# The gated block of a four-block convolution kernel: positions on partitions for the softplus, the delta by rank, two norms side by side

## The reference

```
xn = LN(x) * norm_w + norm_b                      # over the channels of a position
x1, x2 = halves of xn @ w_in.T
xss, z = silu(halves of x1 @ ssm_in_w.T)
xd = xss @ x_proj_w[k].T                          # per direction k = 0..3: 8 dt ranks, 8 B, 8 C
dt = softplus(xd[dt ranks] @ dt_w[k].T + dt_b[k]) # 96 channels for each k
bc = sum over 8 of B * C                          # one number for each position and k
gain = sum over k of (bc * dt + Ds[k])
y = (LN(xss * gain) * out_norm_w + out_norm_b) * z
out = x + (y @ ssm_out_w.T * silu(x2)) @ w_out.T
```

## Time and profile before

| | |
|---|---|
| median of 3 runs | 5742.23 us (5741.26 to 5752.42) |
| the profiled execution | 5744.95 us |
| its span, first to last instruction | 5743.1 us |
| gated block, first product on the image to last addition | 35.6 to 702.8 us |
| PE, DVE, ACT, POOL busy in the span | 87%, 81%, 51%, 67% |
| granted clock of TensorE, mean of the span | 0.94 |

### The profile page before, as it was taken

How to read it: one execution, slowest core, us unless ns; L and a number is a source line. 1 busy time by engine, 2 the same in 40 slices (tenths; PEclk the granted TensorE clock), 3 DMA queues, 4 the chain that set the end, 5 groups by cost and what they waited for, 6 DMA issues and landing times. The chain is left out here.

```text
span 5743.1 us, 74310 instructions
## 1 busy us (share of the span) xinstructions
PE 4971.3 (87%) x16018; PEld 2207.8 (38%) x16018; DVE 4640.4 (81%) x5047; ACT 2949.7 (51%) x4576; POOL 3832.2 (67%) x2568
## 2 busy tenths in 40 slices
PE   6999889897779999998297888888888888888887
PEld 1222256464256666665152222222222222222222
DVE  4876643434418989899797999999999999999996
ACT  5776544443311111111135777777777777777776
POOL 0000032322418898888786999989998999999993
PEclk9998899998889999998698999999999999999998
DMA  2000000001777787776405667667766666677663
GB/s 47 0 0 0 7 1 1 0 1 56 226 158 139 138 152 140 147 141 107 91 9 138 185 183 189 185 182 189 187 186 178 186 185 187 184 189 189 187 184 100
DMA packets 373418, 711.24 MB, mean 124 GB/s; under 512 B 76604, under 2 KB 111224, under 8 KB 358936
## 3 DMA queue, kind: packets, MB, share of 16 engines
q1 hardware_dynamic: 373144, 708.17, 50.2%
HBM read 575.33 MB, written 82.32 MB: 115 GB/s over the span
## 5 line engine op out<-in xcount | busy, mean ns | idle before, releaser
L2015 POOL TENSOR_TENSOR l_hc<-l_h,l_c_rep 128x512 f32<-128x512 f32 x1536 | 1929.8, 1276 | 216.0 <-DVE l_h L2069 187.1
L2069 DVE TENSOR_TENSOR_SCAN l_h<-l_p_da,l_h,l_bu 128x512 f32<-128x512 f32 x1120 | 1412.8, 1279 | 10.5 <-ACT l_p_da L1920 8.8
L1920 ACT ACTIVATE l_p_da<-l_p_da,l_a_neg 128x512 f32<-128x512 f32 x1536 | 1008.5, 658 | 733.8 <-PE l_p_da L1775 712.9
L1221 POOL TENSOR_TENSOR l2b_prod<-l2b_v,l2b_attn 128x1568 f32<-128x1568 f32 x276 | 937.3, 3461 | 242.9 <-DVE l2b_osum L1269 125.2
L1775 PE MATMUL l_p_da<-l_stacked,l_pick 96*128 96x512 f32 x1536 | 908.9, 593 | 191.3 <-DVE l_h L2069 179.1
L2054 DVE TENSOR_TENSOR l_bu<-l_du_rep,l_p_b 128x512 f32<-128x512 f32 x1280 | 855.7, 669 | 29.7 <-DMA l_du_rep<-du_scratch 22.5
L1775 PEld LDWEIGHTS l_p_da<-l_stacked,l_pick 96*128 96x128 f32 x1536 | 293.7, 192 | 1162.4 <-DVE l_h L2069 900.3
L1269 DVE TENSOR_REDUCE l2b_osum<-l2b_prod 128x32 f32<-128x1568 f32 x384 | 665.7, 1780 | 62.9 <-POOL l2b_prod L1221 59.2
L1783 PE MATMUL l_p_y<-l_hc,l_y_pick 128*32 128x512 f32 x3072 | 566.4, 626 | 74.3 <-POOL l_hc L2015 71.7
L1174 ACT ACTIVATE l2b_logits<-l2b_conv,l2b_this_b 98x512 f32<-98x512 f32 x96 | 66.2, 689 | 870.5 <-PE l2b_conv L1139 870.5
L615 POOL TENSOR_TENSOR l_w_pos_low<-l1a_w_sed,l_w_pos_high 96x1536 fp32r<-96x1536 f32 x1 | 4.1, 4123 | 711.2 <-DVE l_w_fc_high L595 711.2
(11 more groups left out here) (267 smaller groups left out, 8905.2 us busy)
## 6 DMA issues: line engine op xcount, KB each, us to landing
l_du_rep<-du_scratch SPq DMA_DIRECT2D x1536, 256.0 KB, 3.8
l2b_img_high<-qkv_scratch SPq DMA_DIRECT2D x192, 306.2 KB, 5.6
l2b_img_low<-qkv_scratch SPq DMA_DIRECT2D x192, 306.2 KB, 9.4
l_stacked<-l_parts SPq DMA_DIRECT2D x512, 96.0 KB, 2.7
l2b_v<-v_scratch SPq DMA_DIRECT2D x192, 152.0 KB, 6.4
qkv_scratch<-l2a_strip SPq DMA_DIRECT2D x32, 840.0 KB, 5.2
du_scratch<-l_du SPq DMA_DIRECT2D x128, 192.0 KB, 2.1
v_scratch<-l2a_v_strip SPq DMA_DIRECT2D x32, 228.0 KB, 4.2
```

Of the source, the lines that this page charges most:

```text
L1221: return eng.tensor_tensor(dst.rearrange("q x (dy dx) -> q x dy dx", dx=WIN), window, attn_half[:, :, unit % 2].rearrange("q x (dy dx) -> ...
L1920: act.activation(p_da[i % DAS][:], p_da[i % DAS][:], ACT.Exp, scale=a_neg[:, k * G + GRP[i]:k * G + GRP[i] + 1]).then_inc(s_da, 1)
L2015: pool.tensor_tensor(hc[:, (G * par + i) % HCS, :], h[:, i, :], c_rep[:, par, :], ALU.mult).then_inc(s_hc, 1)
L2069: dve.tensor_tensor_scan(h[:, i, way], p_da[i % DAS][:, way], of, state, ALU.mult, ALU.add).then_inc(s_h, 1)
```

## The change

Only `gated_ssm_block` and the layout of its weights. Channels stay on partitions for the norms and projections, as before, but:

- The delta goes by rank. One product (`w_bd`, 96 to 96) gives the 32 dt ranks, B and C of the four directions. The ranks are split into a high part (type F32R, copied by ACT and by DVE) and a low part (DVE), stacked with two rows of ones to 98 rows `dtr`; a product takes 128 positions of `dtr` as weights and 384 columns of `w_dt` (4 directions x 96 channels, bias in the last rows), so positions come out on partitions. Four such products a tile, in two pairs.
- relu (DVE) and magnitude (ACT) read these from PSUM in two halves of 128x768; Ln and Exp run over 128x1536; POOL adds the two parts to `dt`.
- bc comes out as one column per direction for 128 positions (four small products of `bc_hl`, split by POOL), and DVE sums over the directions in `chain`: 16 instructions of 128x96, in place in `gain`. Four transposes on PE turn the sum back.
- The norm of x (tile s+2) and that of y (tile s-2) share an instruction each for Square, Ln, Exp and the multiplication; z and g share a Silu. The input norm's weights are multiplied into `w_uzg` with a 97th row for the bias. The output norm's affine and the product with z move to POOL.
- A step s now works from tile s+3 to s-3, and there are 38 steps, from -3 to 34.
- The first image piece is loaded ahead of the weights; the others follow one by one, and PE waits for a piece where its first tile needs it.

The diff, new lines; "..." stands for what is left out, the removed lines (which are in the functions above) among it:

```diff
--- before.py
+++ after.py
@@ -35,14 +35,16 @@
...
+    KS = K * S
+    ROWS_DT = 3 * KS + 2
+    KEEP, GATES = 4, 8
+    CH, CN = 4, N // 4
+    KC = K * C
+    CHAIN = CH * K
+    LAST = TILES + 3
+    FIRST = -3
+    BODY0, BODIES = 5, 3
...
+        bs = sb("l0_bs", [3 * KS, N])
+        bc_hl = sb("l0_bc_hl", [2 * KS, 2, N], F32R)
+        dtr = sb("l0_dtr", [128, N], F32R)
+        relu = sb("l0_relu", [128, 2, CH, KC])
+        sp = sb("l0_sp", [128, 2, CH, KC])
+        dt = sb("l0_dt", [128, CH, KC])
+        gain = sb("l0_gain", [128, CH, C])
...
+        p_c, p_v = ps("l0_p_c", [C, 2, N]), ps("l0_p_v", [C, 2, N])
+        p_u = ps("l0_p_u", [C, N])
+        p_d = ps("l0_p_d", [128, 2, N])
+        p_gain = ps("l0_p_gain", [C, N])
+        p_zg, p_so = p_v, p_d[0:C, 0, :]
+        p_dt = p_d[:, :, 0:KC]
+        p_bc = p_d[:, 1, KC:KC + CHAIN]
...
+            def at(s):
+                step(s, s % GATES, lambda ahead: 0 <= s + ahead < TILES)
+            for s in range(FIRST, BODY0):
+                at(s)
+            with eng.Fori(0, BODIES) as i:
+                for j in range(GATES):
+                    step(GATES * i + BODY0 + j, (BODY0 + j) % GATES, lambda ahead: True)
+            for s in range(BODY0 + BODIES * GATES, LAST):
+                at(s)
...
+        weights = [(center[:], "center"), (mean_w[:], "mean_w"), (w_in1[:], "w_in1"), (ssm_in[:], "ssm_in_T"),
+                   (w_raw[:, 2 * C:], "w_g_T"), (w_bd[:], "w_bd"), (w_dt_full[0:ROWS_DT], "w_dt"),
+                   (rows[0:ROWS_DT], "dt_row_kinds"), (pick_f[:], "pick"), (ident[:], "ident"), (w_so[:], "ssm_out_T"), (w_o[:], "w_out_T"),
+                   (cols[:], "cols")]
...
+            sp_.dma_start(X[:, 0:HW], x[0]).then_inc(s_x, 16)
...
+                sp_.dma_start(dst, w[src]).then_inc(s_w, 16)
+            for b in range(1, B):
+                sp_.wait_ge(s_x, 16 * b)
...
+            pe.matmul(p_u[:, 0:2 * C], w_in1[:], ssm_in[:], start=True, stop=True).then_inc(s_setup, 1)
+            pe.wait_ge(s_setup_cp, 1)
+            pe.matmul(p_gain[0:1, 0:3 * C], cols[:, 1:2], w_raw[:], start=True, stop=True).then_inc(s_setup, 1)
+            pe.wait_ge(s_setup_cp, 6)
+            pe.wait_ge(s_rows, 4)
...
+            def step(s, q, on):
+                if on(-3):
+                    need(pe, s_sgated, s - 2)
+                    pe.matmul(p_so, w_o[:], sgated[:], start=True, stop=True).then_inc(s_o, 1)
+                if on(1):
+                    pe.wait_ge(s_xss, s + 2)
+                    need(pe, s_bcp, s + 1)
+                    pe.matmul(p_u[:], w_bd[:], xss[:, (q + 1) % KEEP, :], start=True, stop=True).then_inc(s_bd, 1)
+                if on(-1):
+                    pe.wait_ge(s_gain, CHAIN * s)
+                    need(pe, s_y, s - 1)
+                    for ch in range(CH):
+                        mm = pe.transpose(p_gain[:, ch * CN:(ch + 1) * CN], gain[:, ch, :], ident[:])
+                    mm.then_inc(s_turn, 1)
+                if on(2) or on(-2):
+                    pe.wait_ge(s_sq, s + 3)
+                    need(pe, s_zg, min(s + 2, TILES) if isinstance(s, int) else s + 2)
+                    if on(2):
+                        mm = pe.matmul(p_v[:, 0, :], mean_w[:], sq[:, 0, :], start=True, stop=True)
+                    if on(-2):
+                        mm = pe.matmul(p_v[:, 1, :], mean_w[:], sq[:, 1, :], start=True, stop=True)
+                    mm.then_inc(s_var, 1)
+                def dt_pair(half):
+                    for j in range(2):
+                        ch = 2 * half + j
+                        mm = pe.matmul(p_dt[:, j, :], dtr[0:ROWS_DT, ch * CN:(ch + 1) * CN], w_dt[0:ROWS_DT],
+                                       start=True, stop=True)
+                    mm.then_inc(s_dtm, 1)
+                if on(1):
+                    pe.wait_ge(s_lo, s + 2)
+                    need(pe, s_out, s - 2)
+                    need(pe, s_bc, s)
+                    dt_pair(0)
+                    pe.wait_ge(s_abs, 2 * s + 3)
+                    dt_pair(1)
+                if on(2):
+                    pe.wait_ge(s_xn, s + 3)
+                    need(pe, s_bcp, s + 2)
+                    pe.matmul(p_u[:], w_uzg[:, 0:C], xn[:, 0, :], start=True, stop=True).then_inc(s_u, 1)
+                    for g in range(2):
+                        mm = pe.matmul(p_zg[:, g, :], w_uzg[:, (g + 1) * C:(g + 2) * C], xn[:, 0, :], start=True, stop=True)
+                    mm.then_inc(s_zgm, 1)
+                if on(1):
+                    pe.wait_ge(s_abs, 2 * s + 4)
+                if on(0):
+                    pe.wait_ge(s_blo, s + 1)
+                    need(pe, s_bc, s)
+                    for ch in range(CH):
+                        mm = pe.matmul(p_bc[:, ch * K:(ch + 1) * K], bc_hl[:, q % 2, ch * CN:(ch + 1) * CN], pick[:],
+                                       start=True, stop=True)
+                    mm.then_inc(s_bcm, 1)
+                if on(3) or on(-1):
+                    need(pe, s_xn, min(s + 3, TILES + 4) if isinstance(s, int) else s + 3)
+                if on(3):
+                    if (q + 3) % GATES == 0:
+                        pe.wait_ge(s_x, (s + 3) * 2 + 16)
+                    pe.nop(nofuse=True)
+                    pe.matmul(p_c[:, 0, :], center[:], X[:, bass.ds((s + 3) * N, N)], start=True, stop=True).then_inc(s_xc, 1)
+                if on(-1):
+                    pe.wait_ge(s_y, s)
+                    pe.matmul(p_c[:, 1, :], center[:], y[:], start=True, stop=True).then_inc(s_yc, 1)
+                if on(-2):
+                    pe.wait_ge(s_yz, s - 1)
+                    need(pe, s_out, s - 2)
+                    pe.matmul(p_so, w_so[:], yz[:], start=True, stop=True).then_inc(s_s, 1)
...
+            def step(s, q, on):
+                par, npar = q % 2, 1 - q % 2
+                if on(1):
+                    act.wait_ge(s_bd, s + 2)
+                    need(act, s_dtm, 2 * s + 2)
+                    act.activation(dtr[0:KS], p_u[0:KS, :], ACT.Copy).then_inc(s_hi, 1)
...
+                if on(2) or on(-2):
+                    both = sides(on, 2, -2)
+                    act.wait_ge(s_var, s + 3)
+                    need(act, s_xn, s + 2)
+                    act.activation(rstd[:, both], p_v[:, both], ACT.Ln, bias=eps[:, 0:1], scale=VAR_SCALE).then_inc(s_ln, 1)
+                    act.wait_ge(s_ln, s + 3)
+                    act.activation(rstd[:, both], rstd[:, both], ACT.Exp, bias=eps[:, 1:2], scale=-0.5).then_inc(s_rstd, 1)
+                def magnitude(half):
+                    act.wait_ge(s_relu, 2 * s + 3 + half)
+                    need(act, s_dt, 2 * s)
+                    act.activation(sp[:, npar, 2 * half:2 * half + 2, :], p_dt, ACT.Abs).then_inc(s_abs, 1)
+                if on(1):
+                    magnitude(0)
+                if on(0):
+                    act.wait_ge(s_exp, s + 1)
+                    act.activation(sp[:, par], sp[:, par], ACT.Ln, bias=1.0).then_inc(s_sp, 1)
+                if on(1):
+                    magnitude(1)
+                    act.wait_ge(s_abs, 2 * s + 4)
+                    act.activation(sp[:, npar], sp[:, npar], ACT.Exp, scale=-1.0).then_inc(s_exp, 1)
+                if on(2):
+                    act.wait_ge(s_u, s + 3)
+                    need(act, s_y, s - 1)
+                    act.activation(xss[:, (q + 2) % KEEP, :], p_u[:], ACT.Silu).then_inc(s_xss, 1)
+                    act.wait_ge(s_zgm, s + 3)
+                    need(act, s_sgated, s - 5)
+                    act.activation(zg[:, (q + 2) % GATES], p_zg[:], ACT.Silu).then_inc(s_zg, 1)
+                if on(3) or on(-1):
+                    both = sides(on, 3, -1)
+                    if on(3):
+                        act.wait_ge(s_xc, s + 4)
+                    if on(-1):
+                        act.wait_ge(s_yc, s)
+                    act.activation(sq[:, both], p_c[:, both], ACT.Square).then_inc(s_sq, 1)
...
+            dve.tensor_copy(w_raw[:, 0:2 * C], p_u[:, 0:2 * C]).then_inc(s_setup_cp, 1)
+            dve.wait_ge(s_setup_cp, 1)
+            dve.tensor_scalar(w_uzg[0:C], w_raw[:], cols[:, 0:1], None, ALU.mult).then_inc(s_setup_cp, 1)
+            dve.wait_ge(s_setup, 2)
+            dve.tensor_copy(w_uzg[C:C + 1], p_gain[0:1, 0:3 * C]).then_inc(s_setup_cp, 1)
+            dve.tensor_copy(pick[:], pick_f[:]).then_inc(s_setup_cp, 1)
+            dve.tensor_reduce(d_sum[:], cols[:, 4:8], AX_X, ALU.add).then_inc(s_setup_cp, 1)
+            dve.tensor_copy(w_dt[0:ROWS_DT], w_dt_full[0:ROWS_DT]).then_inc(s_rows, 1)
...
+            def relu_pair(s, q, half):
+                dve.wait_ge(s_dtm, 2 * s + 3 + half)
+                need(dve, s_dt, 2 * s)
+                dve.tensor_scalar(relu[:, 1 - q % 2, 2 * half:2 * half + 2, :], p_dt, 0.0, None, ALU.max).then_inc(s_relu, 1)
+            def chain(s):
+                dve.wait_ge(s_bcm, s + 1)
+                dve.tensor_copy(bc[:], p_bc).then_inc(s_bc, 1)
```

(75 more changed lines are left out.)

342 lines of the change are left out of this document (64 added, 278 removed).

## The result

The changed kernel takes 5786.15 us (median of 4 runs, 5781.92 to 5790.20), the one before 5745.77 us (4 runs, 5741.26 to 5752.42): 1.0069 times as long, with a 95% interval of 1.0052 to 1.0087, so slower by 0.5 to 0.9%. The profiled execution took 5785.69 us, its span is 5783.9 us.

The account below looks back on a forecast made before the run. PE bounded the old block; in the new one a ring of waits decides. At clock 0.70, 16.4 + 163 + 590 = 770 us against 702.8, 67 us more, gave 5810 us beside the median; range 5690 to 5905.

Parts of the forecast that it names:

- the clock: TensorE's granted clock in the new block, taken as 0.70, between 0.50 and 0.81, because of idle stretches.
- the ring: Waits across engines from one chain's end to the next set the step: 18.6 us at full clock, 9.6 on PE.
- the chain: VectorE's 16 instructions of 128x96 that sum over directions: four at 0.15 and twelve at 0.25, 3.6 us a step.
- rival 1: The block's clock holds at 1.00: 5686 us; chance 0.25, shared with a cheap chain at 0.81 and over.
- Where even lies: The block's clock at which the change would neither win nor lose time: 0.83.
- rival 4: The chain's twelve cost 0.37 each, adding 40 us in all; 0.12 each takes away 45 us; no chance of its own.
- The steps: The block's 26 full steps, 9.0 + 9.6/c each at clock c: 22.7 us at 0.70, 590 us together.
- The ends: The block's 12 steps that aren't full, 100 + 44/c at clock c: 163 us at 0.70.
- The start: With the first image loaded ahead of the weights, the first product comes at 16.4 us instead of 35.6.
- What stood behind the block: The kernel's other stages, not touched by the change and taken as they are.
- Rival 3: The block's clock never recovers from 0.50, with transposes not counting as busy: 5980 us; chance 0.12, with worse than 0.57.
- unknown ones: GpSimd's affine and copy, without a row there: each between 0.1 and 1.4 us, taken as 1.0.

Follow-up runs that it names:

- e4: The changed kernel with two unused f32 products of 512 columns between the two delta pairs; 5686.4 us.
- e6: e2 with small products ahead of the variances, softplus logarithm earlier, ordinary products for the transposes, ScalarE's table load ahead of its copy of the ranks; 5679.7 us.
- e3: The changed kernel with its four transposes a step made as ordinary f32 products with the identity matrix; 5760.9 us.
- e5: The changed kernel with two unused f32 products between the delta pairs and two more ahead of the wait for the chain; 5726.0 us.
- e9: e6 with two unused f32 products of 512 columns between the two delta pairs; 5654.6 us.
- e12: e6 with unused products (two between the delta pairs, one ahead of u), output product ahead of the variances, ScalarE's copy ahead of its table load; 5596.6 us.
- e11: The changed kernel with twelve unused transposes between the two delta pairs; 5775.0 us.
- e2: The changed kernel with sgated behind the chain, the output product and its addition later, GpSimd's dt additions first; 5739.4 us.

## Why the prediction was right, and where its sizes were off

**Slower, by the clock and the ring: right.** The forecast was 5810 and its reason that no engine is full, that DVE waits for s with the chain behind it, and that PE's stretches of idling bring the clock to 0.70; the block had 0.69, and the wait for s is DVE's longest. The experiments bear out both halves. e4 has the same order and more work, so that its 100 us can only come from the clock: with the clock up the change is faster than the kernel before. A step of e4 at full clock takes 17.4 us, where a tile of before took 18.9. That e4's 5686.4 is also rival 1's number is chance, since rival 1 took a clock of 1.00 and a longer ring. e6 changes the order, and the transposes with it (worth 25 by themselves), and wins 106.

That the clock came out at 0.69 for 0.70 is in part luck. The choice was a judgement between 0.50 and 0.81, and it took no account of the long dips with PE busy, which are seven of 16 in the changed kernel. Where even lies (0.83 in the forecast) wasn't measured: e3, with the same order and 0.78, ended its block 20 us after the old one, and e4 and e5, with 0.88 and 0.84, ended theirs 54 and 8 us before it, but with two and four unused products a step.

**The ring.** From e4's step: chain ended at 408.2, transposes done at +0.7, variances at +2.4 (I had 2.9), u begun at +6.9 (7.3), g done at +9.7 (10.1), small ones at +10.2 (11.0), s at +12.9 (14.1). From copy to copy it is 17.4 us where I had 18.6; DVE in that step of e4:

```profile
404.40 0.16 DVE L317 COPY l_bc<-l_p_d 128x16 f32<-128x16 f32 x1
404.68 0.81 DVE L325 TENSOR_SCALAR l_gain<-l_dt,l_bc 128x96 f32<-128x96 f32 x4
405.41 2.83 DVE L328 SCALAR_TENSOR_TENSOR l_gain<-l_dt,l_bc,l_gain 128x96 f32<-128x96 f32 x12
...
421.81 0.16 DVE L317 COPY l_bc<-l_p_d 128x16 f32<-128x16 f32 x1
```

Three terms of the sum were too large: transposes 0.64 for 0.92, small products 0.60 for 0.9, centerings and s 2.7 for 3.06. The transposes had a reason: their row, 0.92 for four, is from the stretch of the earlier trace rows with a clock of 0.50, and the sum took it as a time at full clock. The delta pair, which is not in this sum, was too small, 0.6 to 0.7 for 0.5. PE has 8.5 of the 17.4, the others 8.9 (I had 9.0). The chain is right at 3.56 us, from the start of its first four to the end of the last twelve, here in the changed kernel:

```profile
208.15 0.69 DVE L358 TENSOR_TENSOR l_sgated<-l_p_d,l_zg 96x512 f32<-96x512 f32 x1 [10.91 <-PE l_p_d L226]
208.75 0.16 DVE L311 COPY l_bc<-l_p_d 128x16 f32<-128x16 f32 x1
209.39 0.81 DVE L319 TENSOR_SCALAR l_gain<-l_dt,l_bc 128x96 f32<-128x96 f32 x4 [0.48 <-DVE l_bc L311]
210.11 2.84 DVE L322 SCALAR_TENSOR_TENSOR l_gain<-l_dt,l_bc,l_gain 128x96 f32<-128x96 f32 x12
```

The twelve, the form without a row, take 2.84 us, 0.24 each, where I had 0.25; rival 4 fell both ways.

**The steps.** From the copy of tile 3 to that of tile 29 of the changed kernel there are 26 steps, 22.05 us each, against 22.7, which is 17 us less in all:

```profile
120.24 0.16 DVE L311 COPY l_bc<-l_p_d 128x16 f32<-128x16 f32 x1
...
693.42 0.16 DVE L311 COPY l_bc<-l_p_d 128x16 f32<-128x16 f32 x1
```

The form of the sum is less right than its result. With the measured terms, 8.9 + 8.5/c, a step at 0.69 would take 21.2 us and not 22.05. The mean clock counts stretches at full clock in which PE only waits, while u, z and g, which lie on the ring, began at half clock in every step. So the terms that were too large made up for a mean clock that was too kind.

**The ends** took 160.6 us for 163. **The start** was at 18.5 for 16.4: the weights behind the first image landed at 13.2 and not 11.5. Sum 752.3 for 770, and the whole -17.7 from there.

**What stood behind the block** was taken as untouched. From the start of the block's last addition to the end it was 8.7 us shorter, 5032.3 for 5041.0 us. The code there is the same in all these kernels, and this time ran from 5028.3 (e9) to 5041.0 (e12) with no relation to what the block did; it is an uncertainty of the sum, and its cause is open. With the 17.7 it makes the 26 us between 5812 and 5785.69.

**Of the clock** the forecast said that u, z and g would run slow in most steps. u took 1.99 to 2.02 us in every one of them; z and g were through earlier in some, as the clock came back. Rival 3 (never recovers) fell: the clock came back within the step shown, at 266.9 us, and behind the long dips too. Its reason, the transposes, was half right: e3 and e11 give them little weight, but in the step shown the variances behind them ran at full clock. And its row is weaker than it was read: from 1703 to 1709 us transposes fill the first 3.8 us, and split products of 512 columns the rest.

**Of the waits** the forecast named as PE's longest those for the chain and for the B times C product. From 200 to 600 us they were 21.2 and 8.4 us, and the longest was that for the magnitude, 45.9. The prediction had that wait in its part on the clock and not among the signs.

**GpSimd.** Its unknown ones were 0.77 and 0.60 us, under the 1.0 taken, and its terms add up to 8.3 us and not 9.5; the trace has 7.4 a tile. It was never late: it waited for xn, 14.6 us a step. So the slip decided nothing.

## What to carry to other kernels

A change that takes work off the engine that bounds a stage can lose if it leaves that engine waiting: price the new ring of waits from end to end, and price the engine's products at the clock that the idle stretches will leave it. Look for what one engine has queued behind a wait for another; here the moves of e2 and e6, with ordinary products for the transposes, took 3.5 us off a step. Where TensorE must idle between bursts, ordinary products for transposes can pay, and even unused ones in the gap, but not where what stands behind them is on the ring.

## What was not expected of the hardware

Two unused products, together 1.96 us a step at full clock, raised the granted clock of a block from 0.69 to 0.88 and took 100 of 5786 us off the kernel. Four of them where PE was busy already raised the clock as well (0.83): the dip behind the idle stretch stayed in each step, and the long dips went. Four transposes in place of four ordinary products, 0.64 us for 1.04, cost 0.09 of the block's clock. And filling a second stretch left the clock lower than filling one (0.84 against 0.88), by fewer but longer dips; in the one shown, and in the step ahead of it, PE was nearly always busy. Why it began is open.
